# Softplus additions as accumulating transfers, one more product on GpSimd, and a new order of every queue in a selective-scan kernel

## The reference

```python
def selective_scan(u, dt, A, Bm, Cm, Dp):
    def step(h, inp):
        u_t, dt_t, B_t, C_t = inp
        dA = jnp.exp(dt_t[:, :, None] * A)
        h = dA * h + (dt_t * u_t)[:, :, None] * B_t[:, None, :]
        y = jnp.einsum('bin,bn->bi', h, C_t)
        return (h, y)
...
def mamba_layer(x, p):
    h = rmsnorm(x, nw)
    u, z = jnp.split(jnp.einsum('blh,ch->blc', h, in_w), 2, axis=-1)
    u = jax.nn.silu(causal_conv(u, cw, cb))
    proj = jnp.einsum('bli,ci->blc', u, xp_w)
    dt_r, Bm, Cm = (proj[..., :R], proj[..., R:R + N], proj[..., R + N:])
    dt = jax.nn.softplus(jnp.einsum('blr,ir->bli', dt_r, dtw) + dtb)
    y = selective_scan(u, dt, -jnp.exp(a_log), Bm, Cm, dp) * jax.nn.silu(z)
    return x + jnp.einsum('bli,hi->blh', y, ow)
```

## Time and profile before

| | |
|---|---|
| median of three runs | 14675.39 us (14674.05 to 14681.67) |
| the profiled execution's own time | 14673.68 us |
| its span | 14671.9 us |
| scans run | from 296.8 us to 13,400 us of the span, 256 units |
| one unit in steady state | 51.20 us |
| busy in the span | POOL 89%, DVE 90%, PE 87%, ACT 78% |

### The profile page before, as it was taken

The page is one execution under the profiler, slowest core; times in us unless marked ns, Lnnn a source line. Parts: engine busy times, 40 slices in busy tenths (PEclk is TensorE's granted clock), DMA queues, the critical chain, the costliest instruction groups (busy, mean ns, idle before and its releaser), DMA issues. The chain is left out here.

```text
span 14671.9 us, 199619 instructions
## 1 busy us (share of the span) xinstructions
PE 12767.7 (87%) x51482; PEld 6493.1 (44%) x51482; DVE 13198.2 (90%) x8949; ACT 11448.7 (78%) x21760; POOL 13105.2 (89%) x6096
## 2 busy tenths in 40 slices
PE   7888888888888888888888888888888888888989
PEld 4444444444444444444444444444444444444667
DVE  3999999999999999999999999999999999997323
ACT  4888888888888888888888888888888888886111
POOL 2999999999999999999999999999999999995033
PEclk8998889998889998889998889998889998888799
DMA  3333333333333333333333333333333333332022
GB/s 91 115 123 122 124 119 115 121 118 126 122 120 116 118 120 119 129 115 121 115 123 120 126 118 115 121 117 126 121 123 115 119 118 122 125 118 90 21 64 57
DMA packets 677527, 1660.68 MB, mean 113 GB/s; under 512 B 84687, under 2 KB 331856, under 8 KB 677196
## 3 DMA queue, kind: packets, MB, share of 16 engines
q1 hardware_dynamic: 656712, 1642.87, 33.1%
q0 software_dynamic: 19968, 15.98, 0.7%
q10 hardware_dynamic: 720, 0.55, 0.0%
HBM read 1372.64 MB, written 286.41 MB: 113 GB/s over the span
## 5 line engine op out<-in xcount | busy, mean ns | idle before, releaser
L908 POOL TENSOR_TENSOR dbu<-dtu_rep,b_rep 128x972 f32<-128x972 f32 x4096 | 9122.9, 2255 | 284.6 <-DVE h L842 273.2
L842 DVE TENSOR_TENSOR_SCAN h<-ps,dbu 128x972 f32<-128x972 f32 x4096 | 8856.5, 2173 | 269.7 <-ACT ps L643 260.6
L643 ACT ACTIVATE ps<-dt_rep,A_cur 128x323 f32<-128x323 f32 x12288 | 5842.4, 520 | 323.0 <-DVE h L842 311.1
L851 DVE TENSOR_TENSOR h<-h,ps 128x972 f32<-128x972 f32 x3585 | 4094.4, 1142 | 0.0
L478 PE MATMUL ps<-h,fold 128*32 128x486 f32 x16400 | 3528.4, 719 | 0.4 <-DVE h L851 0.4
L556 PE MATMUL ps<-u_raw,w_cv 128*128 128x162 f32 (+7 forms) x8256 | 1827.0, 374 | 170.1 <-ACT u_raw L679 168.8
L556 PEld LDWEIGHTS ps<-u_raw,w_cv 128*128 128x128 f32 x8256 | 1337.3, 190 | 714.6 <-ACT u_raw L679 299.1
L478 PEld LDWEIGHTS ps<-h,fold 128*32 128x32 f32 x16400 | 714.7, 128 | 1873.5 <-issue 1872.2
L576 PE MATMUL ps<-u_act,w_x 128*128 128x324 f32 x1548 | 855.8, 723 | 516.6 <-ACT u_act L694 509.7
L465 PE MATMUL ps<-c_rows,sel_c 16*128 16x324 f32 x2048 | 827.1, 483 | 375.0 <-DVE h L851 374.9
L916 POOL TENSOR_TENSOR h<-h,c_rep 128x972 f32<-128x972 f32 x513 | 1150.3, 2242 | 0.0
(11 more groups left out here) (189 smaller groups left out, 14184.1 us busy)
## 6 DMA issues: line engine op xcount, KB each, us to landing
dt_rep<-dt_rows SPq DMA_DIRECT2D x1028, 486.0 KB, 4.6
dtu_rep<-dtu_rows SPq DMA_DIRECT2D x1028, 486.0 KB, 4.9
b_rep<-b_rows SPq DMA_DIRECT2D x1028, 162.0 KB, 4.8
dt_rows<-dt SPq DMA_DIRECT2D x257, 486.0 KB, 2.7
dtu_rows<-dtu SPq DMA_DIRECT2D x257, 486.0 KB, 3.0
c_rep<-b_rows SPq DMA_DIRECT2D x513, 162.0 KB, 3.6
w_cv<-in_w_cv SPq DMA_DIRECT2D x17, 768.0 KB, 7.1
b_rows<-xp_rows SPq DMA_DIRECT2D x258, 40.5 KB, 4.7
```

What stands on the lines that cost most here:

```text
L643: ins = act.activation(decay[s % 2][:, it * L + 1:(it + 1) * L], dt_rep[:, s % NR, it, 1:L], ACT.Exp, scale=A_cur[:, it * N + s:it * N + s ...
L842: dve.tensor_tensor_scan(h[s % RING][:, :, :].rearrange("p i t -> p (i t)"), decay[s % 2], dbu[s % DRING][:, :, :].rearrange("p i t -> p ( ...
L851: dve.tensor_tensor(h[s % RING][:, :, :], h[s % RING][:, :, :], c_ps.unsqueeze(1).broadcast_to([128, IT, L]), ALU.mult).then_inc(s_prod, 1)
L908: pool.tensor_tensor(dbu[s % DRING][:, :, :], dtu_rep[:, r, :, :], b_rep[:, q, :].unsqueeze(1).broadcast_to([128, IT, L]), ALU.mult).then_ ...
```

## The change

`ON_POOL` becomes (3, 7, 12) where it was (4, 12): three products of a unit are POOL's and 13 DVE's, and `c_rep` and its semaphores get a third slot. The first three steps of `ge_dt` are no longer instructions of POOL but transfers that it issues, which add to `dt` on landing; they must follow one another, so each waits for the one before through `s_acc` (16 for each that has landed). The order of the terms is now exp, ln, correction, and the correction is written with the other sign. Whoever waited for `s_dt` now waits for all three transfers of the unit (48 a unit): the copy of the convolution into `u_pre` and the copy of `dt`, too. All five lists of calls are put in another order.

```diff
-ON_POOL = (4, 12)
+ON_POOL = (3, 7, 12)
...
@@ se_conv (half 0) and se_softplus (step 2)
-                reached(act, s_dt, 4 * k - 2)
+                wait(act, s_acc, 48 * k)
...
-                act.activation(u_pre[:, :], u_pre[:, :], ACT.Identity, bias=cst["minus_one"][:, 0:1]).then_inc(s_sp, 1)
+                act.activation(u_pre[:, :], u_pre[:, :], ACT.Identity, bias=cst["one"][:, 0:1], scale=-1.0).then_inc(s_sp, 1)
...
@@ ge_dt
-            if step == 0:
-                reached(pool, s_sp, 4 * p + 1)
-                pool.tensor_tensor(dt[:, :], dt[:, :], exp_x[:, :], ALU.add).then_inc(s_dt, 1)
-            elif step == 1:
...
+            if step < 3:
+                term, ready, at = ((exp_x, 1, 0), (u_pre, 4, 2), (dtu, 2, 1))[step]
+                reached(pool, s_sp, 4 * p + ready)
+                wait(pool, s_acc, 16 * (3 * p + at))
+                pool.sem_inc(s_held, 1)
+                pool.dma_start(dt[:, :], term[:, :], accum_op=ALU.add).then_inc(s_acc, 16)
             else:
-                reached(pool, s_dt, 4 * p + 3)
+                wait(pool, s_acc, 16 * (3 * p + 3))
                 reached(pool, s_ua, p + 1)
-                pool.tensor_tensor(dtu[:, :], dt[:, :], u_act[par][:, :, :].rearrange("p i t -> p (i t)"), ALU.mult).then_inc(s_dt, 1)
+                pool.tensor_tensor(dtu[:, :], dt[:, :], u_act[par][:, :, :].rearrange("p i t -> p (i t)"), ALU.mult).then_inc(s_dtu, 1)
...
@@ tensor_step
             if scan:
+                te_sum(pe, u, 0)
                 te_out(pe, u, 0)
-                te_sum(pe, u, 0)
+                te_bcast(pe, u, par, 1)
                 te_out(pe, u, 1)
-                te_bcast(pe, u, par, 1)
...
                 te_sum(pe, u, 2)
+            if a1:
+                te_xp(pe, k, par)
+            if scan:
                 te_sum(pe, u, 3)
             if a1:
-                te_xp(pe, k, par)
...
@@ sync_step: load_c has a third slot, the stores and the loads of b move
```

More of the change, by code:

```diff
@@ L413, in run_layers @@
         s_sp = sem("s_sp")
-        s_dt = sem("s_dt")
+        s_dtu = sem("s_dtu")
+        s_acc = sem("s_acc")
         s_cq = sem("s_cq")
@@ L617, in tensor_step @@
             if a1:
+                te_conv(pe, k, 0)
                 te_conv(pe, k, 1)
@@ L750, in se_softplus @@
             elif step == 2:
-                reached(act, s_dt, 4 * p - 2)
+                wait(act, s_acc, 48 * p)
                 reached(act, s_ua, p + 1)
@@ L780, in scalar_step @@
                 se_decay(act, u, 2)
+                se_decay(act, u, 3)
             if b1:
                 se_z(act, p, 0)
-            if scan:
-                se_decay(act, u, 3)
-            if b1:
+                se_softplus(act, p, 2)
                 se_z(act, p, 1)
-                se_c_rows(act, p, other)
-                se_softplus(act, p, 2)
             if scan:
@@ L796, in scalar_step @@
             if scan:
-                se_decay(act, u, 6)
                 se_out(act, u, 1)
+            if b1:
+                se_c_rows(act, p, other)
+            se_copy_nw(act, j)
+            if scan:
                 se_decay(act, u, 7)
-            se_copy_nw(act, j)
+            se_sq(act, j + 1)
             if a1:
+                se_copy_cb(act, k)
                 se_ur(act, k, 0)
@@ L804, in scalar_step @@
                 se_decay(act, u, 8)
[L805 to L808, removed]
+            se_rstd(act, j)
             if scan:
@@ L811, in scalar_step @@
             if a1:
-                se_conv(act, k, 0)
-                se_copy_cb(act, k)
+                se_ur(act, k, 1)
             if scan:
                 se_decay(act, u, 10)
+            se_weighted_x(act, j, other)
+            if a1:
+                se_conv(act, k, 0)
+            if scan:
                 se_decay(act, u, 11)
+                se_decay(act, u, 12)
             if a1:
                 se_conv(act, k, 1)
-            if scan:
-                se_decay(act, u, 12)
-            if a1:
                 se_silu(act, k, par, b1)
@@ L947, in gpsimd_step @@
                 ge_dbu(pool, u, 0)
+            if b1:
+                ge_dt(pool, p, 1 - par, 0)
+            if scan:
                 ge_dbu(pool, u, 1)
@@ L958, in gpsimd_step @@
                 ge_dbu(pool, u, 8)
+                ge_product(pool, u, 3)
+                ge_dbu(pool, u, 9)
             if b1:
@@ L961, in gpsimd_step @@
             if scan:
-                ge_dbu(pool, u, 9)
-                ge_product(pool, u, 4)
-            if b1:
-                ge_dt(pool, p, 1 - par, 2)
-            if scan:
                 ge_dbu(pool, u, 10)
+                ge_product(pool, u, 7)
             if b1:
@@ L971, in gpsimd_step @@
                 ge_dbu(pool, u, 11)
+            ge_x_norm(pool, u + 3, 1 - par)
+            if scan:
                 ge_dbu(pool, u, 12)
@@ L1006, in sp_store_dt @@
         def sp_store_dt(sp, p, which):
-            reached(sp, s_dt, 4 * p + 3 + which)
+            if which:
+                reached(sp, s_dtu, p + 1)
+            else:
+                wait(sp, s_acc, 16 * (3 * p + 3))
             sp.sem_inc(s_go, 1)
@@ L1032, in sync_step @@
             if b1:
+                sp_load_b(sp, u, par, 0)
+            if scan:
+                sp_load_c(sp, u, par, 2)
+            if b1:
                 sp_store_dt(sp, p, 0)
@@ L1036, in sync_step @@
             if b1:
+                sp_load_c(sp, p, 1 - par, 0)
+                sp_load_c(sp, p, 1 - par, 1)
+                sp_load_b(sp, u, par, 1)
                 sp_store_dt(sp, p, 1)
@@ L1040, in sync_step @@
             if b1:
-                sp_load_b(sp, u, par, 0)
-            if scan:
-                sp_load_c(sp, u, par, 1)
-            if b1:
+                sp_load_b(sp, u, par, 2)
                 sp_load_dt(sp, u, 0)
```

26 lines of the change are left out of this document (7 added, 19 removed).

## The result

The changed kernel takes 14768.26 us (14763.03 to 14776.83, four runs), the kernel before on the same chip 14674.72 (14671.53 to 14681.67): ratio 1.0064 [1.0051, 1.0077]. It is slower by 0.6%, where I had forecast 14330, and it lies outside the range of 14220 to 14650.

A forecast was written before the change was run, and what follows sets the result against it. The prediction took DVE and POOL, both nearly always busy, to bound the kernel together. DVE's 48.5 us of work plus a 1.34 wait made 49.85 us a unit against 51.20, times 256 346 us less: 14330 us, range 14220 to 14650.

The forecast's parts named there:

- A product less on DVE: DVE does 13 products instead of 14, 1.06 us less: a floor of 48.5 us a unit with small gaps.
- The gate behind product 1: DVE's 0.91 us wait ahead of the gate is filled by product 1 and goes, at a price of 0.
- POOL: POOL does two operations less, 45.6 us, plus three transfer issues at 1.30 each: 49.5 us, fitting barely in the unit.
- Rival 2: Issues cost POOL what it was relieved of: 51.2 us a unit at the scatter's price, 14675 to 14700; chance 0.12.
- Landing: The third transfer lands 5.4 us after issue, POOL's multiplication reaches it after 5.7: no stall.
- Rival 3: The third transfer lands late and stalls POOL; slower from a 7.4 us landing on, 15260 at 9.7; chance 0.12.
- Scan 13's wait: On DVE, from scan 10's end to scan 13 8.70 us against 7.36 of work: a wait of 1.34, 0.75 more.
- Does TensorE deliver the convolution in time?: TensorE's convolution ends at about 34.3 us from scan 0's start, decay 12 at 34.25: they meet to a tenth.
- the sign that xp would come without a wait: Sign to check in TensorE's profile after: xp comes with no wait ahead of it.
- I keep that price: TensorE's sum ahead of the gate stays at 3.20 us, against 1.82 elsewhere, for the lower clock.
- rival 1: TensorE's chain is late, the lower clock costing 1.38 us in a third to half of units: 14470; chance 0.18.
- The chances: Chances given for the measured outcome: faster 0.77, same 0.08, slower 0.15.

The follow-up runs named there:

- e14: e9 with product 3 back on DVE and the broadcast for steps 4 to 7 behind the second output half: 14682.58 us, 1.0005 to the kernel before.
- e4: The changed kernel with the three accumulating transfers left out, POOL only counting the semaphore up: 14752.95 us, 1.005 to the kernel before.
- e9: e5 with 11 idle products instead of 5 behind the old unit's sum: 14325.06 us, 0.973 to the kernel before.
- e11: The changed kernel, nothing moved, with idle products (zero weights) in five of TensorE's waits: 14609.08 us, 0.9922 to the kernel before.
- e7: The kernel before, nothing moved, with idle products at four of TensorE's waits: 14678.33 us, 1.0004 to the kernel before.
- e6: e2 with sum 3 back ahead of xp beside sum 2, no idle products: 14529.23 us, 0.99 to the kernel before.
- e8: The changed kernel with product 3 back on DVE, POOL keeping 7 and 12: 15401.66 us, 1.0495 to the kernel before.
- e12: The changed kernel with TensorE's and ScalarE's lists in the order of before: 15064.39 us, 1.0233 to the kernel before.
- e2: The changed kernel with one skip product half ahead of the broadcast, one between the convolution's halves: 14651.83 us, 0.998 to the kernel before.
- e5: e2 with idle products in three of TensorE's waits, 5 of them behind the old unit's sum: 14491.74 us, 0.9871 to the kernel before.
- e10: e9 with sum 3 back ahead of xp beside sum 2: 14732.12 us, 1.0007 to the kernel before.
- e1: The changed kernel with both halves of the skip product ahead of the broadcast and the convolution: 14699.33 us, 1.0012 to the kernel before.
- e13: The kernel before, nothing moved, with idle products at six of TensorE's waits: 14678.99 us, 1.0001 to the kernel before.
- e3: The changed kernel, orders kept, with idle products in TensorE's waits: 14699.51 us, 1.0011 to the kernel before.

## Why the prediction was wrong

By its own steps:

- *A product less on DVE*, −1.06: right. e14 shows 1.1 at full clock.
- *The gate behind product 1*, its wait gone at no price: right in the short units.
- *POOL*: right in direction. The issue was taken at 1.30 start to start and costs 0.61, so POOL ends up with slack and waits for exp. Rival 2 is out.
- *Landing*: taken 5.4, with no stall. The three have medians of 4.5 to 5.7, and over all 771 the median is 4.7 and the longest 9.0. Rival 3 is out, and e4 confirms it. The Trainium skill's fit (DMA: Bandwidth & Descriptors, Anatomy of one DMA — SWDGE path), an estimate of 3.1 us for 486 KB, doesn't agree with the 4.7 seen for accumulating transfers.
- *Scan 13's wait*: forecast 1.34, measured 1.52, but the stretch behind it was counted 8.70 us and measured 9.73, 1.03 more; scan 12's wait of 0.68 hides most of that in the comparison. In e9, where silu follows its copy at once, the stretch is 8.61 and the wait 1.17. So the terms of the count were good, and one was missing: the step said that silu waits only for its copy. **This is the step that failed, together with the next one.**
- *Does TensorE deliver the convolution in time?* It does, to the tenth, but the question stopped at the convolution. Silu waits for three things, and the last, the skip product, starts where the convolution ends: 1.80 us in TensorE's order, 1.15 of it beyond the copy. Sum 2 behind it holds up scan 12 by 0.68. With scan 2's 0.27, the unit at 7000.40 has 1.13 us more of waits than forecast. The 0.27 is not this step's: that unit's clock is 0.93, and in e11, near full clock, scan 2 does not wait and the unit takes 50.63. So the order costs about 0.8 us a unit over the forecast's 49.85. For the same reason the sign that xp would come without a wait did not come true: it waits 1.37 for silu. The wait on `s_skip` was in the listing and had no row among the waits before, since it was hidden; I looked only at waits that the trace showed.
- *"I keep that price"*, for the lower clock at one place, and rival 1 (0.18). The place moved and others came. Rival 1 had the mechanism, but took it as a correction to a good kernel. Its price was 1.38 a piece; the 69 long units are 2.2 us longer than the others, and average out to 0.60 a unit (51.46 − 50.86). The short units lose some 0.2 to the clock as well (50.86 against e11's 50.63).
- *The chances*: by the list of rivals they add up to 0.76 for faster and 0.16 for slower, not 0.77 and 0.15.

The sum with the measured terms: 49.85 + about 0.8 for the waits behind the convolution + about 0.8 for the clock (0.60 of it in the long units) = 51.46, and before it is 51.17. Two kernels whose TensorE is kept near full clock (0.97 and 0.98 in the mean) show the parts in another way: filling the waits takes the kernel after from 1.0064 to 0.9922 (e11), the skip product's new place, with the idle products put where that order waits, takes it to 0.973 (e9). With both gone, a unit is 49.56 us and the kernel 14325 us, against 49.85 and 14330 forecast. So the forecast describes a kernel whose skip product is out of the way and whose TensorE is at full clock. That the two times come so close is chance: the unit is 0.29 us shorter than forecast, 0.17 of it at scan 13, which makes 74 us, and the part behind the last gate, which the forecast took as unchanged, is 61 us longer than in the profile of before. By ratio the forecast was 0.9765 and e9 is 0.973.

The 24 us behind the last gate aren't from the change's own code. The first 200 us there, in the kernel before and in the kernel after:

```profile
13415.50:13615.50 200.00, 165.18 (x767) 119.60 (x766) 104.03 (x259) 80.05 (x172) 0.00 (x0) 0.83 0.17 45
```

```profile
13488.40:13688.40 200.00, 164.37 (x657) 115.95 (x656) 92.55 (x219) 74.84 (x157) 0.00 (x0) 0.73 0.14 40
```

The granted clock is 0.83 in one and 0.73 in the other, in the same part of the program. Why it is lower wasn't tested; e9 has the lower one too.

What stays open: what the kernel before takes at full clock, and so how much of e9's 2.7% belongs to the change and how much to the idle products. By the estimate from e7, about 0.6 us a unit (50.2 against 49.56) would be the change's and 1.0 the clock's, but no kernel in this record shows the 50.2 in every unit. e6, which has no idle products, shows 1.0% for the change with the skip product moved and sum 3 back. Why so many versions come to the same 51.2 us (below) is open too.

## What to carry to other kernels

When an edit brings a producer and a consumer to meet, go through every semaphore that the consumer waits for, the ones that release a buffer for overwriting too; a wait that costs nothing before has no row in the trace, only in the code. In these traces TensorE often paid twice for a wait of a microsecond or two, once for the wait and once for the slow work behind it: look at the windows behind its waits before an order is judged, and put independent work, or an idle product, in there. And an order belongs to the split of the work that it was made for: half of a change (e8, e12) was far worse than either whole.

## What the runs showed of the hardware

- Work that does nothing made the kernel faster: 20 products with zero weights a unit (11 + 7 + 2) raised the mean granted clock from 0.906 (e2) to 0.977 and took 2.5 points off the ratio (0.998 to 0.973).
- Behind single waits of 0.9 to 2.0 us, in a TensorE that is otherwise 88% busy, the granted clock fell to its lower level, 1.2 GHz: 0.92 in the kernel after (the slow convolution), 1.88 ahead of xp in e2, 1.64 in e5 (eight instructions in 3.45 us instead of 1.91), 2.02 in e10. Not every such wait did it: in e6 xp took 1.90 us behind a wait of 1.86. The Trainium skill (TensorE: Matmul & The Clock Gate, "A second HAM failure mode: psum-queue depth-cycling") describes a clock that goes up and down with short, frequent idling between groups of matmuls; the traces here agree, with mean granted clocks of 0.86 to 0.92 in the kernels without idle products.
- Four kernels with different orders, the one before, e1, e10 and e13, take 51.2 us in nearly every unit, and e3, e7 and e14, whose units are of two kinds, average 51.18 all the same. In the units of the first four that I compared, the waits and the slow pieces stand in the same place. It looks as if the loop's length locks on to the clock's changes; that was only seen, not tested.
- An accumulating transfer of 486 KB within the core's memory held POOL for 0.61 us and landed in a median of 4.7 us; POOL's operations had longer records throughout that kernel, not only behind an issue (dbu 2.55 us in the mean against 2.26 before and in e4 2.25), and still 2.20 us start to start. So their sum of busy time is no measure of POOL's load there.
